# Expert weights loaded as three 2 MB transfers per expert in place of six of 1 MB

## The reference

```python
x = x + cross(layernorm(x), ctx_2048, mask)
xn = layernorm(x)                                   # 4096 x 1024
Xp = xn[slots_token].reshape(32, 160, 1024)         # gather: each expert's tokens
G = einsum('ecd,edi->eci', Xp, W_gate)              # W_gate: 32 x 1024 x 512, f32 (2 MB per expert)
U = einsum('ecd,edi->eci', Xp, W_up)                # W_up:   32 x 1024 x 512
Y = einsum('eci,eid->ecd', silu(G) * U, W_down)     # W_down: 32 x 512 x 1024
out = zeros.at[slots_token].add(Y * slots_w)        # scatter-add
out = x + out + shared(xn)
```

## Time and profile before

| | us |
|---|---|
| median of 3 runs | 1971.4 (1969.09 to 1972.84) |
| the profiled execution: time | 1967.85 |
| its span in the profile | 1966.2 |
| PE busy | 1827.7 (93% of the span) |
| DVE busy | 1373.2 (70%) |
| ACT busy | 865.1 (44%) |
| first expert's products begin | 1281.92 |

### The profile page before, as it was taken

One profiled execution on the slowest core, in us unless ns is written; L12 is line 12 of the kernel. 1 busy time (PEld: TensorE's weight loads), 2 busy tenths in 40 slices (PEclk: granted clock), 3 DMA queues, 4 the chain that ended last, 5 costly groups with the idle time before them and its releaser, 6 DMA issues.

```text
span 1966.2 us, 44131 instructions
## 1 busy us (share of the span) xinstructions
PE 1827.7 (93%) x17428; PEld 1398.4 (71%) x17428; DVE 1373.2 (70%) x2509; ACT 865.1 (44%) x1210; POOL 609.7 (31%) x618
## 2 busy tenths in 40 slices
PE   0059999999999999999999999999999999999997
PEld 0037767767866866866876776788888888888886
DVE  5999667557557557556644644588888888888884
ACT  8664212112122122221221211367777777777774
POOL 2200220221122022022022012456556556556552
PEclk9989999999999999999999999999999999999999
DMA  9963542443434344343243155499999999999993
GB/s 377 408 206 106 129 119 55 120 108 73 110 98 92 92 106 100 87 108 97 55 108 97 33 117 158 124 346 353 367 363 349 367 370 347 366 366 356 359 367 89
DMA packets 188529, 395.51 MB, mean 201 GB/s; under 512 B 116400, under 2 KB 120528, under 8 KB 163824
## 3 DMA queue, kind: packets, MB, share of 16 engines
q1 hardware_dynamic: 163264, 334.77, 49.5%
q0 software_dynamic: 23952, 58.81, 13.6%
q10 hardware_dynamic: 1184, 0.15, 0.0%
HBM read 314.79 MB, written 55.35 MB: 188 GB/s over the span
## 4 chain that ended last, share of the span: by engine, by line
PE 85%; issue 3%; DVE 2%; POOL 1%; DMA 1%; ACT 0%; SPq 0%; POOLq 0%; ACTq 0%
PE ps L1382 52%; PE ps L1395 14%; PE ps L1593 8%; PE ps L1420 5%; PE ps L1601 2%; PE ps L1456 1%; DVE W L1067 1%; PE ps L1515 1%; POOL slots L575 1%; DMA FR<-xn_rows,gix 0%; PE ps L1461 0%; PE ps L1479 0%; PE ps L1521 0%; DVE st L1083 0%; ACT W L719 0%
## 5 line engine op out<-in xcount | busy, mean ns | idle before, releaser
L1382 PE MATMUL ps<-XT,W 128*128 128x256 f16 (+1 forms) x12192 | 1098.9, 252 | 5.0 <-issue 3.0
L1382 PEld LDWEIGHTS ps<-XT,W 128*128 128x128 f16 x12192 | 1014.4, 98 | 87.3 <-issue 15.3
L1326 DVE SCALAR_TENSOR_TENSOR W<-BIG,W 128x2048 f16<-128x2048 f32 x192 | 436.1, 2286 | 64.1 <-ACT W L890 64.1
L890 ACT ACTIVATE W<-BIG 128x2048 f16<-128x2048 f32 x192 | 361.4, 1900 | 0.0
L1395 PE MATMUL ps<-W,HH 128*128 128x512 f16 x1536 | 334.6, 379 | 2.3 <-DVE X L1220 1.2
L830 ACT ACTIVATE SG<-ps 128x256 f32<-128x256 f32 x128 | 49.1, 384 | 635.5 <-PE ps L1382 627.8
L1395 PEld LDWEIGHTS ps<-W,HH 128*128 128x128 f16 x1536 | 150.3, 98 | 183.5 <-DVE X L1220 1.7
L263 POOL TENSOR_TENSOR expo<-expo 128x1 f32<-128x1 f32 x160 | 85.9, 537 | 598.4 <-ACT FR L761 274.2
L1236 DVE SCALAR_TENSOR_TENSOR SG<-ps,SG 128x256 f32<-128x256 f32 x128 | 54.4, 425 | 248.8 <-ACT SG L830 248.6
L568 POOL TENSOR_TENSOR rs<-ve,expo 128x1 f32<-128x1 f32 x32 | 17.6, 551 | 577.7 <-DVE ve L1087 577.7
L622 POOL DMA_INDIRECT FR<-xn_rows,gix x64 | 172.9, 2701 | 29.9 <-issue 29.9
(11 more groups left out here) (192 smaller groups left out, 1631.5 us busy)
## 6 DMA issues: line engine op xcount, KB each, us to landing
BIG<-in_w_gate SPq DMA_DIRECT2D x64, 1024.0 KB, 8.9
BIG<-in_w_up SPq DMA_DIRECT2D x64, 1024.0 KB, 7.6
BIG<-in_w_down SPq DMA_DIRECT2D x64, 1024.0 KB, 8.1
X<-in_x SPq DMA_DIRECT2D x16, 1024.0 KB, 5.0
X<-in_mask POOLq DMA_DIRECT2D x16, 1024.0 KB, 8.2
xn_rows<-FR SPq DMA_DIRECT2D x32, 512.0 KB, 3.5
out_rows<-X SPq DMA_DIRECT2D x32, 512.0 KB, 3.6
W<-in_x SPq DMA_DIRECT2D x6, 2048.0 KB, 22.5
```

The lines of the kernel that those rows point to most:

```text
L890: ac.activation(dst, stage, ACT.Copy, scale=W_SCALE).then_inc(x_hi, 1)
L1326: ve.scalar_tensor_tensor(out=lo[cut], in0=src, scalar=W_SCALE, in1=hi[cut], op0=ALU.mult, op1=ALU.subtract).then_inc(x_lo, 1)
L1382: ins = te.matmul(out_ps, a[:, k, cols], b[:, k, :], start=n == 0, stop=n == len(steps) - 1)
```

## The change

Three loads per expert replace six. Each fetches both halves of one matrix, 256 rows of 8 KB in memory, into two neighbouring stages: a partition gets two runs of 8 KB that lie 1 MB apart in memory. There is one semaphore per matrix. The load waits until both stages are free, and ACT waits for the whole 2 MB before it splits either half.

```diff
-        ld_ew = [sem(f"ld_ew{m}") for m in range(6)]
+        ld_ew = [sem(f"ld_ew{m}") for m in range(3)]
...
             def ew_load(e, m):
-                src = rows((w_gate, w_up, w_down)[m // 2], (e * 2 + m % 2) * P, P)
-                sp.dma_start(ew_stage[m], src).then_inc(ld_ew[m], 16)
+                src = rows((w_gate, w_up, w_down)[m], e * 2 * P, 2 * P)
+                sp.dma_start(BIG[:, 8192 * m:8192 * (m + 1)].bitcast(F32).rearrange("p (t f) -> p t f", t=2),
+                             src.rearrange("(t p) f -> p t f", p=P)).then_inc(ld_ew[m], 16)
...
-                        for m in (2 * j, 2 * j + 1):
-                            sp.wait_ge(x_lo, m + 1)
-                            ew_load(1, m)
+                        sp.wait_ge(x_lo, 2 * j + 2)
+                        ew_load(1, j)
...
-            for m in range(6):
-                if m == 5:
+            for m in range(3):
+                if m == 2:
 
                     sp.wait_ge(t_xn, 64 * (GROUPS - 1))
                 ew_load(0, m)
...
-            for m in (4, 5):
-                sp.wait_ge(x_lo, m + 1)
-                ew_load(1, m)
+            sp.wait_ge(x_lo, 6)
+            ew_load(1, 2)
             with sp.Fori(2, E) as e:
-                for m in range(6):
-
-                    wait(sp, x_lo, e * 6 + (m - 5))
+                for m in range(3):
+
+                    wait(sp, x_lo, e * 6 + (2 * m - 4))
                     ew_load(e, m)
...
             def ew_hi(e, b, m, first=False):
-                act.wait_ge(ld_ew[m], e * 16 + 16)
+                act.wait_ge(ld_ew[m // 2], e * 16 + 16)
```

## The result

The change makes the kernel slower by a third of a per cent: 1979.01 us (median of 8 runs, 1975.88 to 1982.39) against 1972.88 (8 runs, 1969.09 to 1973.51), ratio 1.0035, interval 1.0026 to 1.0043. By the ratio that is 6.9 us; the two medians lie 6.1 apart. The profiled execution of the change took 1982.39 us with a span of 1980.8, which is its slowest; it lies 14.6 us above the span of before, of which 2.8 us were there when the first expert's products began (1284.73 against 1281.92). The expert stage is what to compare.

A forecast was written before the change was run, and what follows sets the result against it. PE was taken to bound the expert stage. One late up load plus small stalls summed to +2.3 us: 1967.85 + 2.3 = 1970.2 for the profiled execution, 1973.7 for the median; range 1968.5 to 1989.

The forecast's parts named there:

- What bounds the stage and what the change spends: Expert stage: PE bounds it and no load is late; the change spends the loads' slack of about 7 us.
- U: The up matrix's load in an expert: slack 1.5 us in one expert, 0.3 in the next, the tight one.
- D: The down matrix's load, next in the queue after the up load: lands at 1635.3, slack 2.1 us.
- G: The gate matrix's load, after the down load and ahead of the next up load: lands at 1641.5, slack 1.5 us.
- the 1.8 that I had allowed for it: ACT's idle time before two waits for PE, 1.04 + 0.74 us, by which the down load may be late.
- The chain from a late U to PE: Up load, ACT's activations of chunk 2, DVE's low part, PE's down product: lateness d stops PE for d - 0.1.
- the tolerance: Between the end of DVE's low part and PE's down product: at most 0.3 us apart, counted as 0.1.
- Three loads fewer cost or bring nothing of their own: SP issues three DMAs fewer per expert and executes three waits fewer: 0, as SP spends its time waiting.
- forecast or no stall: Expert stage: a +2.3 us stall, or slack holding everywhere at 1971.4, taken as one case; chance 0.50.
- the late U: Rival: the up load is late in every expert and stops PE; about +12 us, 1983, chance 0.42.
- what two halves took there, one load of two halves takes now: Queue speed in the expert stage: a merged load takes the time two halves took there in the landings of before.
- The stall is paid once: Expert stage: one stall of 2.1 us near 1354 moves all later needs and issues; small ones follow, together 0.2.

The follow-up runs named there:

- merge_up: Against the kernel before, only the up matrix comes in one load of 2 MB, gate and down stay in two each: 1979.97 us, ratio 1.0038.
- merge_gate_down: Against the kernel before, gate and down come in one load of 2 MB each, up stays in two: 1971.87 us, ratio 0.9997.
- the third profile: The change itself, unaltered, measured and profiled a third time against the kernel before: 1981.03 us, ratio 1.0046.
- up_early: The change, with DVE making the low part of half 3 earlier so the up load is issued earlier: 1974.32 us, ratio 1.0008 against before.
- six-transfer twin: The waits of the change with six transfers of 1 MB, against the kernel before: 1976.58 us, ratio 1.0023; again 1976.13 us, 1.0021.
- late_six: The kernel before, six loads of 1 MB, each first half issued only when the second may be: 1973.05 us, ratio 1.0003.

## Why the prediction was right, and where its sum was off

- *What bounds the stage and what the change spends.* Right. PE had no idle time, and the only new idle time is behind loads. The means of all instructions stayed.
- *U is the tight one, D and G are not.* Right, shown by merge_up (1.0038) and merge_gate_down (0.9997). D was late by up to 0.6 in 12 experts, in the third profile by up to 1.4 in 14, inside the 1.8 that I had allowed for it, and PE didn't feel it.
- *The chain from a late U to PE, with next to no slack.* Right: 3.66 became 3.25, and the other seven lost 0.3 to 0.4 as well, so that is the tolerance, not 0.1.
- *G lands at 1641.5, about 2.7 us after the issue of U.* Right for the late experts: 1.9 to 3.5 us in the three profiles of the change.
- *Three loads fewer cost or bring nothing of their own.* Nearly: up_early is level with before. The difference between the change and its six-transfer twin, some 2 to 5 us, stays open.
- *The size: +2.3 us.* Mis-sized. It measured +6.9. That is beyond the 3.9 us that I had set as the least that can be told from no change, so the case held likeliest (forecast or no stall, 0.50) did not come about. The time lies inside the whole range only because that was widened for the late U. This rival gave the sign and was closer in kind, but it is not every expert that is late. The term that failed is "what two halves took there, one load of two halves takes now", and it failed by its spread and not by its usual value. I had U land 9.1 us after its issue (1617.7 to 1626.8), with 6.6 and 7.6 us from landing to landing; the 24 fully recorded loads in time took 9.25 us in the median, and 5.7 to 7.5 us (median 6.0) after the landing of G. In the late experts the whole U took 7.7 to 10.8 us after the landing of G, and 10.6 to 13.9 after its issue, for a part or a few that came behind the others. My sum had no term for this; only the argument for the rival named it, as the engines that wait for the slowest of them. late_six bears it out: a late second half is wanted 3.1 us later there, and nothing waits for it.
- *The stall is paid once.* Half right. Needs and issues do move with a stall, but late loads also follow one another (those issued at 1326.4 and 1348.6, at 1563.6 and 1586.7), and the stalls come back over the whole stage: 9, 7 and 8 waits for the up load in three profiles, most of them of about 1 us. My working used one execution's landings as if they were the same each time, and so left out the scatter from expert to expert, which 7 us of slack had covered. Eight stalls of PE, 1.1 us in the mean, are the sum in place of one of 2.1 and small ones of 0.2.

On the rule that was weighed, from the Trainium skill, page "DMA: Bandwidth & Descriptors", section "Latency and other measured facts" (a large power of two as the pitch between partitions slows copies), the measurement decides against carrying it over to runs within a partition: merge_gate_down, with such runs in two loads of three, is at 0.9997.

What stays open is why one transfer of 2 MB did worse than two of 1 MB under the same waits, and why in about a quarter of the experts a part of the up load is behind the rest, up to 11 to 14 us after the issue.

## What to carry to other kernels

Before loads are merged, work out for each one the time from the issue, which moves to that of its last part, to the need, which stays that of its first; where another engine is full, the load with the least of it decides, and the others can be merged for nothing. The landing times of one expert give the usual landing of a merged load (9.1 us worked out, 9.25 measured) and not its spread: a load has landed only with the last of its 16 parts, so the slack has to cover the slowest part, here up to 13.9 us. Where a merged load is short of time, look for the instruction that frees its buffer: moved ahead of its neighbour on an engine with idle time, it gave back all of the loss but what can't be told from none (1.0008, 0.9999 to 1.0017).

## What the runs showed that I had not expected

- With DMA at a share of 1.00, a late issue costs nothing as such: late_six issues as late as the change and is level with before (1.0003).
- In the change the DMA share falls below one half in the microsecond after the issue of the up load in only 3, 4 and 2 of 28 experts of the three profiles, fewer than are late, and what made ACT wait was one part in 16, sometimes two or three.
- Taking the reads out of the scatter-add lowered the DMA share from 1.00 to 0.92 and left the lateness of the up load as it was (11.6 us in 11 waits, against 12.0 in 9).
- One profile of a kernel can lack a gap that nearly all its executions seem to have (ACT's 8.7 us near 1250): it stood in one of two profiles of before, and in the profiles of all twelve other runs.
